# An attention and expert pipeline with one first-pass tile moved ahead, merged transfers, and pass-2 masks moved from TensorE to two GpSimd fills a head

## The reference

```python
proj = qkv @ in_proj.T + in_proj_bias                 # 16 heads of 16 columns
scores = einsum('bhqd,bhkd->bhqk', q, k) * SCALE + (k - q) * alibi_slopes
scores = where(pos_k > pos_q, -inf, scores)           # causal
attn = maximum(softmax(scores, axis=-1), 1e-10)
s = (attn @ v, heads joined) @ out_w.T + out_b
# experts: rms norm, router softmax, top 4 of 32 experts, up to 128 rows each,
# silu(x w_gate) * (x w_up) @ w_down, weighted and added per row;
# a shared expert (704 wide) for every row, times a sigmoid; plus the input
x = x + s * silu(experts)
```

## Time and profile before

| | us |
|---|---|
| median of 3 runs | 638.89 |
| lowest and highest run | 635.98, 642.01 |
| the profiled execution | 641.21 |
| its span, first to last instruction | 639.6 |

### The profile page before, as it was taken

The page is one execution under the profiler, slowest core; times in us unless marked ns, Lnnn a source line. Parts: engine busy times, 40 slices in busy tenths (PEclk is TensorE's granted clock), DMA queues, the critical chain, the costliest instruction groups (busy, mean ns, idle before and its releaser), DMA issues.

```text
span 639.6 us, 17284 instructions
## 1 busy us (share of the span) xinstructions
PE 564.7 (88%) x4583; PEld 386.8 (60%) x4584; DVE 489.6 (77%) x1098; ACT 445.3 (70%) x1021; POOL 263.8 (41%) x632
## 2 busy tenths in 40 slices
PE   1699559778998999999999999999999998999994
PEld 1594227545665666666666666666666665666663
DVE  5988963668778778886887788778878885788556
ACT  1412574268877778887888788888878886788670
POOL 7630000215445355445544564455355445344403
PEclk9959869799999999999999999999999999999998
DMA  8992255553335333533543344335334346731157
GB/s 243 179 241 76 97 156 167 136 161 60 91 84 111 86 92 87 107 89 90 102 104 98 87 102 90 87 84 116 90 89 102 92 103 200 167 80 24 16 146 136
DMA packets 79538, 71.47 MB, mean 112 GB/s; under 512 B 18115, under 2 KB 70021, under 8 KB 79493
## 3 DMA queue, kind: packets, MB, share of 16 engines
q1 hardware_dynamic: 70292, 59.30, 34.1%
q0 software_dynamic: 9136, 11.80, 12.3%
q10 hardware_dynamic: 80, 0.03, 0.0%
HBM read 47.82 MB, written 23.59 MB: 112 GB/s over the span
## 4 chain that ended last, share of the span: by engine, by line
PE 50%; ACT 14%; issue 11%; DVE 10%; DMA 7%; SPq 6%; ACTq 1%; POOL 1%; POOLq 0%; DVEq 0%
ACT PSB L1062 7%; PE PSB L897 6%; PE PSB L765 6%; PE PSB L791 6%; ACT PB L1071 5%; PE PSB L889 5%; PE PSB L813 5%; PE PSB L810 4%; PE PSB L868 4%; PE PSB L787 3%; SPq L497 2%; PE PSB L666 2%; PE PSB L761 2%; PE PSB L850 2%; DVE WDS L1277 2%
## 5 line engine op out<-in xcount | busy, mean ns | idle before, releaser
L1342 DVE TENSOR_REDUCE NEGM<-PSB 128x1 f32<-128x1024 f32 (+7 forms) x256 | 192.3, 752 | 64.4 <-PE PSB L765 62.5
L1062 ACT ACTIVATE PSB<-PSB,NEGM 128x1024 f32<-128x1024 f32 (+7 forms) x256 | 182.5, 713 | 33.3 <-DVE NEGM L1342 33.0
L1071 ACT ACTIVATE PB<-PSB 128x128 f32<-128x128 f32 (+7 forms) x256 | 166.3, 651 | 43.7 <-PE PSB L791 41.6
L1348 DVE TENSOR_SCALAR PB<-PB 128x128 f32<-128x128 f32 (+7 forms) x256 | 116.9, 466 | 26.5 <-ACT PB L1071 24.1
L765 PE MATMUL PSB<-STACKS 111*128 111x512 bf16 (+3 forms) x384 | 106.6, 332 | 0.0
L791 PE MATMUL PSB<-STACKS 111*128 111x512 bf16 (+3 forms) x384 | 104.3, 326 | 0.0
L787 PE MATMUL PSB<-MK,IDB 128*128 128x128 bf16 x256 | 57.5, 225 | 21.2 <-ACT PSB L1062 13.7
L1660 POOL DMA_INDIRECT moe_rows<-YE,IDX x32 | 57.3, 1792 | 29.2 <-issue 29.2
L810 PE MATMUL PSB<-PB,VH 128*32 128x256 f32 x640 | 68.3, 387 | 0.0
L787 PEld LDWEIGHTS PSB<-MK,IDB 128*128 128x128 bf16 x256 | 24.5, 96 | 58.4 <-ACT PB L1071 31.5
L761 PE MATMUL PSB<-MQ,IDB 128*128 128x128 bf16 x256 | 58.3, 228 | 1.1 <-ACT UL L1049 0.5
(11 more groups left out here) (199 smaller groups left out, 1169.4 us busy)
## 6 DMA issues: line engine op xcount, KB each, us to landing
STACKS<-q_parts SPq DMA_DIRECT2D x192, 32.0 KB, 1.8
STACKS<-k_parts SPq DMA_DIRECT2D x192, 32.0 KB, 1.8
WGU<-in_L_ffn_w_gate_dram SPq DMA_DIRECT2D x32, 176.0 KB
WGU<-in_L_ffn_w_up_dram SPq DMA_DIRECT2D x32, 176.0 KB
WDS<-in_L_ffn_w_down_dram SPq DMA_DIRECT2D x32, 176.0 KB
...
```

The costliest lines, as they stand in the source:

```text
L1062: act.activation(sc, sc, ACT.Exp, bias=NEGM[:, par, i:i + 1], accum_out=LSUM[:, par, i:i + 1]).then_inc(exp1_done, 1)
L1071: act.activation(PB[:, k % 2, prob_offset(s):prob_offset(s) + (s + 1) * P], psf[:, base:base + (s + 1) * P], ACT.Exp).then_inc(exp2_done, 1)
L1342: dve.tensor_reduce(NEGM[:, par, i:i + 1], psf[:, base:base + (i + 1) * P], AX_X, ALU.max, negate=True).then_inc(max_ready, 1)
L1348: dve.tensor_scalar(p, p, FLOOR, 0.0, ALU.subtract, ALU.max).then_inc(clamp_done, 1)
```

## The change

It has several parts.

- TensorE, VectorE and ScalarE: in phases that have all three units, pass 1 of step 1 (896 columns) comes in step 0, after pass 2 of step 0 and ahead of the value products; the maximum and the exponential likewise.
- The copy to XET goes from VectorE to ScalarE, in step 2, ahead of the exponential.
- The seed exponential comes in step 0 instead of step 1; transpose and copy of the shift come in step 4 instead of step 5.
- The mask of pass 2 is written by TensorE only for step 7. For the other seven tiles GpSimd fills the upper part of the diagonal tile with zeros in the clamped probabilities, in two selects a head: tiles 0 to 3 (after the clamp of step 3) and tiles 4 to 6 (after the clamp of step 6). The tiles of PB are laid out anew so that the diagonal tiles of a fill have one stride. The first batch of value products waits for the fills instead of for the clamp.
- Transfers: three loads and one per operand instead of six and one; one store of the shift rows instead of three, now ahead of the heads; the copy of the input to the output in eight pieces spread over the pipeline (`copy_x`); `load_again` in five pieces in phases 25 to 29.
- GpSimd gathers before it prepares the values.

```diff
 def prob_offset(s):
-    return s * (s + 1) // 2 * P
+    return 9 * P * s if s < NQ // 2 else P * (10 * (NQ - 1 - s) + 1)
+def diagonal(probs, tiles):
+    n = len(tiles)
+    if tiles.start < NQ // 2:
+        first, step, at = prob_offset(tiles.start), 9 * P, 0
+    else:
+        first, step, at = prob_offset(tiles[-1]) - 9 * P, 10 * P, 9 * P
+    return probs[:, first:first + step * n].rearrange("p (n c) -> p n c", c=step)[:, :, at:at + P]
+FILLED = (range(0, 4), range(4, 7))
...
+                for first, parts, times in runs:
+                    n = parts * times
+                    src = one[first:first + parts]
+                    if times > 1:
+                        src = src.broadcast_to([n, DH, S])
+                    sp.dma_start(t[r * DH:(r + n) * DH, :], src).then_inc(semaphore, 16)
...
-                load_operand(QS[slot], q_parts, (0, 1, 2, 0, 1, 0), q_alibi, u_head, u, stack_loaded[slot])
+                load_operand(QS[slot], q_parts, ((0, 3, 1), (0, 2, 1), (0, 1, 1)), q_alibi, u_head, u, stack_loaded[slot])
...
+                if exists(it, k + 1):
+                    store_shift(it, k + 1)
                 if exists(it, k - 1):
                     store_heads(it, k - 1)
-                if exists(it, k + 1):
-                    store_shift(it, k + 1)
-                if isinstance(it, int) and k == DIRECT + 1:
-                    load_again(0)
-                if isinstance(it, int) and k == DIRECT + 2:
-                    load_again(1)
+                if k >= 2 and k % SLOTS == 2:
+                    copy_x(it, k)
+                if isinstance(it, int) and k in AGAIN:
+                    load_again(k)
...
-                for a in range(3):
-                    sp.dma_start(rows[SHIFT + a:SHIFT + a + 1, :].rearrange("o (t q) -> o t q", q=P),
-                                 CT[NQ * a:NQ * a + NQ, :]).then_inc(c_rows_ready, 16)
+                sp.dma_start(rows[SHIFT:SHIFT + 3, :], CT[:, :]).then_inc(c_rows_ready, 16)
...
+            def copy_x(it, k):
+                rows = bass.ds(turn(it, k, SLOTS, P), P)
+                sp.dma_start(out[0][rows, :], x[0][rows, :]).then_inc(x_again[0], 16)
...
-                pe.matmul(psf[:, base:base + P], IDB[:, :], MK[:, :],
-                          start=True, stop=False, skip_group_check=True)
+                masked = s == NQ - 1
+                if masked:
+                    pe.matmul(psf[:, base:base + P], IDB[:, :], MK[:, :],
+                              start=True, stop=False, skip_group_check=True)
...
-                pe.wait_ge(clamp_done, unit(it, k, NQ, VALUE_BATCH[batch][-1] + 1))
+                if batch == 0:
+                    pe.wait_ge(fill_done, unit(it, k, len(FILLED), len(FILLED)))
+                else:
+                    pe.wait_ge(clamp_done, unit(it, k, NQ, NQ))
...
-                    if exists(it, k + 2):
+                    ahead = exists(it, k + 2) and exists(it, k - 1)
+                    if exists(it, k + 2) and not (s == 1 and ahead):
                         pass1(it, k + 2, s)
                     if exists(it, k):
                         pass2(it, k, s, exists(it, k + 2))
+                    if s == 0 and ahead:
+                        pass1(it, k + 2, 1)
...
-                    if s == 5 and exists(it, k + 1):
+                    if s == 4 and exists(it, k + 1):
                         c_transpose(it, k + 1)
...
+                    if s == 2 and exists(it, w):
+                        o = aux_task(it, w, TR)
+                        act.activation(XET[:, :, :].rearrange("p c m -> p (c m)"), o[:, 0:D], ACT.Copy)\
+                            .then_inc(xet_ready, 1)
...
+                    if s == 1 and ahead:
+                        exp1(it, k + 2, s)
                     if exists(it, k):
                         exp2(it, k, s, exists(it, k + 2))
-                    if s == 0 and isinstance(it, int) and k == UNITS - 2:
+                    if s == 0 and exists(it, k + 1):
                         exp_seed(it, k + 1)
...
+            def fill_diagonal(it, k, part):
+                tiles = FILLED[part]
+                hold(pool, clamp_done, unit(it, k, NQ, tiles[-1] + 1))
+                d = diagonal(PB[:, k % 2, :], tiles)
+                pool.affine_select(out=d, in_=d, compare_op=ALU.is_ge, fill=0.0, base=0,
+                                   pattern=[[0, len(tiles)], [1, P]], channel_multiplier=-1).then_inc(fill_done, 1)
...
+                if exists(it, w + 1):
+                    gather(it, w + 1)
                 if exists(it, k + 1):
                     prepare_values(it, k + 1)
-                if exists(it, w + 1):
-                    gather(it, w + 1)
+                if exists(it, k):
+                    fill_diagonal(it, k, 0)
...
+                if exists(it, k):
+                    fill_diagonal(it, k, 1)
```

63 lines of the change are left out of this document (31 added, 32 removed).

## The result

The changed kernel takes 634.3 us (median of 7 runs) where the kernel before, measured beside it, takes 639.7. The ratio is 0.9914, interval 0.9888 to 0.9941: 5.5 us faster by that ratio (5.4 by the two medians), where 15.4 were forecast (638.9 to 623.5). A second measurement on another occasion gave 634.0 and 0.9915 (0.9882 to 0.9948).

A forecast was written before the change was run, and what follows sets the result against it. A TensorE-ScalarE wait chain bounds ordinary phases, TensorE alone long ones. Gains 6.7 (ordinary), 3.7 (long), 1.3 (outer masks), 5.0 (transfers), less 0.7 (tail): 16.0 off 638.9, 0.6 given back: 623.5 us, range 611 to 639.

The forecast's parts named there:

- Masks on TensorE: Pass 2, seven of eight mask products leave TensorE: 0.25 us gained per ordinary phase, 0.44 per long one.
- Long phase: Every fourth phase, bound by TensorE alone: all seven masks count (0.44), plus 0.02 at step 0; 0.46 us gained.
- The 896-column tile ahead: Step 0 of ordinary phases: 0.13 us gained before pass 2, less 0.08 waiting for the last exponential; 0.07 net.
- Copy of the expert rows on ScalarE: Step 2: some 0.37 us moves to ScalarE, not ahead of step 3's maximum, within a 0.5 us reserve; no charge.
- Shift rows transposed in step 4: Transpose moves from step 5, so shift rows are stored about 3 us before pass 2 needs them; no cost charged.
- Seed earlier: Softmax seed exponential moves into ScalarE's wait for the first maximum; GpSimd's chain starts some 3.5 us earlier.
- Fills 0.6 and 0.5: GpSimd's two zero fills per phase take 0.6 and 0.5 us, with room for them; nothing charged in the loop.
- Rival 3: GpSimd becomes the bound once fill time per phase (F) reaches 3.3 us; slower, 647 us, chance 0.10.
- Transfers: Merged loads and copies in pieces take back 5.0 us of late transfers, bounds 0 and 6.4.
- Tail: End of kernel: the last unit's values wait for an uncovered fill, 0.65 us longer.
- rival 2: Loop gains nothing in ordinary phases, the moved tile waiting for the last exponential: 632.6 us, chance 0.20 with its neighbourhood.
- the ring: Chain of TensorE, step 3's tile, maximum and exponential, then ScalarE and TensorE, taken to set ordinary phases at 14.53 us.

The follow-up runs named there:

- best: Changed kernel without the tile ahead, expert-row copy on VectorE, shift rows turned in step 5, first expert loads held for gathered rows, last unit's masks on TensorE: 621.99 us.
- no_ahead: Changed kernel with pass 1 of step 1 (the 896-column tile) back in step 1 on all three engines: 632.21 us.
- transfers_only: Kernel before with only SyncE's part of the change (merged loads, one shift-row store, input copy and reload in pieces): 636.59 us.

## Why the prediction was wrong

The direction was right, the size was 2.8 times too large. Step by step:

- *Masks on TensorE, 0.25 per ordinary phase and 0.44 per long one*: right, 1.06 measured for 1.19. (One mask is 0.06 us by the two starts in the earlier trace rows; the fourth digit of 0.0625 is in no row.)
- *Long phase*: "TensorE is the bound, so all seven masks count". It shrank by 0.16 (16.23 to 16.07), not 0.46. In best it is 15.82 with TensorE busy for 15.82; in the changed kernel the moves opened gaps of 0.14 in it.
- *The 896-column tile ahead, +0.07*: wrong in sign; it costs 0.49 per four phases. The 0.13 that I added, the gap before pass 2 of step 0, is gained without the tile as well: in no_ahead pass 2 of step 0 starts at the same 0.20 us before the first maximum as in the changed kernel. I had credited it to the wrong edit. The transfers alone close it: in transfers_only these scores start 0.14 before the first maximum, where they start 0.02 before it in the earlier trace rows:

```profile
307.27 0.22 PE L802 MATMUL PSB<-STACKS 111*128 111x128 bf16 x1
```
```profile
307.41 1.23 DVE L1353 TENSOR_REDUCE NEGM<-PSB 128x1 f32<-128x1024 f32 x1 [0.79 <-PE PSB L776]
```

  And the phase that I measured, 14.53, is the longest of the three ordinary ones (14.30, 14.53, 14.35); in the first of them the scores already started 0.24 before the maximum, so there was less to gain than three times 0.13: transfers_only gains 0.17 in all four. The loss by the tile's wait for the last exponential, which I had put at 0.08, is 0.13 at its start, mostly taken up again at step 4. The larger loss, 0.28 in the first ordinary phase, I had not seen: the tile's exponential stands ahead of the one that pass 2 of step 2 waits for.
- *Copy of the expert rows on ScalarE, free*: "neither stands ahead of the maximum of step 3". True, and the wrong question: it stands ahead of the exponential of step 3, through two others in ScalarE's queue. Beside the tile ahead this costs nothing (59.12 and 59.10), alone 0.24.
- *Shift rows transposed in step 4, free*: I looked only at when they are stored, and not at what they displace. They stand ahead of pass 1 of step 5 on TensorE at the start of ScalarE's dense stretch, which costs 0.56 per four phases, the largest of the three as they were taken back here.
- *Seed earlier*: the place in ScalarE's wait is right (310.31, in the idle time before 311.21). But I priced it at nothing, and it is what makes the fills possible.
- *Fills 0.6 and 0.5, no wait for them in the loop*: right. The groups of the changed kernel by form (count, busy, mean ns):

```profile
L1586 POOL TENSOR_SCALAR_AFFINE_SELECT PB<-PB 128x512 f32<-128x512 f32 x32 | 21.1, 659 | 6.7 <-DVE PB L1384 6.7
L1586 POOL TENSOR_SCALAR_AFFINE_SELECT PB<-PB 128x384 f32<-128x384 f32 x32 | 16.9, 528 | 45.0 <-DVE PB L1384 44.5
```

- *Rival 3, GpSimd as the bound from F = 3.3*: the threshold lies lower. Twice the fills, F = 2.3, already make the values wait and lengthen ordinary phases by up to 0.5 us (the stalls at the loop's turn left aside), and with the seed one step later single ones are too much. An average over GpSimd's round is the wrong measure for an engine whose work is pinned at both ends, here by the seed and by the clamps.
- *Transfers, 5.0*: right, 4.6 measured (interval 2.7 to 6.5). Its step "SyncE's queue empties several us earlier" had a price of its own: from the issue of the first gather to the second unit's first maximum 15.99 us before (119.79 to 135.78) and 17.46 now (117.97 to 135.43), with a gather that took 6.7 us instead of 3.6.
- *Tail, +0.65*: 1.83 us of wait where 0.70 was, so 1.13. Its own terms (622.53 + 0.1 + 0.5, against 622.68) give 0.45, or 0.6 with the start's own delay; the fill took 0.82, not 0.5.

The sum of the loop shows it best. A gain of the size that was forecast, 1.42 per four phases, is there: best has 57.80 against 59.41, and 1.44 of these 1.61 go beyond transfers_only. It is not made up as forecast, though: the masks measured 1.06 with the moves in place, and what brings the rest of the 1.44 (the masks without the moves, the earlier seed, the order on GpSimd) no run separates. The change gives 1.30 of the 1.61 back; taken one after the other on the way from best, the copy 0.25 (to 58.05), the shift rows 0.56 (to 58.61) and the tile 0.49 (to 59.10). Seven and a half times 1.30 is 9.8 us over the loop's 30 phases, and the two ends give some 3 more. By the medians the step is 12 us (634.0 to 622.0), but the kernel before was 4.3 us faster beside best; by the ratios, 0.9915 and 0.9779, it is some 9. The loop's part is sure: from the second unit's first maximum to the last one that both traces show, 439.48 us (135.43 to 574.91) and 429.73 (132.75 to 562.48), 9.75 less.

The step that failed is thus the pricing of the three moves: the tile ahead at +0.07 a phase and the copy and the shift rows at nothing, where they cost 0.49, 0.25 and 0.56 per four phases. That the result is near what rival 2 had (632.6) is chance: of its way, the wait for the last exponential, some 0.1 per phase is there and mostly taken up again. Three operations were set ahead of something that the ring waits for.
